# Workspace FFN: reload of x behind its residual sum, loads signalled in halves, output summed in a ring of four first rows

## The reference

```python
for _ in range(2):
    logits = rms(x, norm_pre_w) @ compete_w.T + compete_b
    vals, idx = top_k(swap(logits), 4)
    written = softmax(vals) @ gather(x @ write_w.T + write_b, idx)
    ws = rms(ws + written, norm_post_w)            # 16 slots a batch
    q = x @ wq.T + bq; kk = ws @ wk.T + bk; vv = ws @ wv.T + bv
    x = rms(x + attention(q, kk, vv) @ out_w.T + out_b, norm_post_w)
```

## Time and profile before

| | before |
|---|---|
| median of three runs | 4041.53 us |
| the profiled execution's own time | 4037.83 us |
| its span | 4036.0 us |
| mean granted TensorE clock | 0.972 of full speed |
| PE busy | 3624.9 us (90%) |
| DVE busy | 2861.6 us (71%) |
| ACT busy | 2582.2 us (64%) |
| POOL busy | 1597.4 us (40%) |
| last stage | from about 3024 us to the end |

### The profile page before, as it was taken

How to read it: one execution, slowest core, us unless ns; L and a number is a source line. 1 busy time by engine, 2 the same in 40 slices (tenths; PEclk the granted TensorE clock), 3 DMA queues, 4 the chain that set the end, 5 groups by cost and what they waited for, 6 DMA issues and landing times. The chain is left out here.

```text
span 4036.0 us, 86194 instructions
## 1 busy us (share of the span) xinstructions
PE 3624.9 (90%) x24451; PEld 1808.3 (45%) x24451; DVE 2861.6 (71%) x4477; ACT 2582.2 (64%) x6419; POOL 1597.4 (40%) x2090
## 2 busy tenths in 40 slices
PE   5999999999999996699999799999976988889896
PEld 1222222222222221577778544444444654655563
DVE  5888888888888885577777577777764455444545
ACT  2777777777777775577777577777762534445353
POOL 6444444444444440666666122222221242332323
PEclk9999999999999998799999999999998999999998
DMA  7777777777777762333333133333323030120202
GB/s 113 125 120 125 120 125 120 125 120 124 120 125 121 123 107 72 103 113 113 112 113 115 58 93 93 93 94 94 94 74 110 1 126 2 64 65 33 95 1 79
DMA packets 342550, 385.82 MB, mean 96 GB/s; under 512 B 58432, under 2 KB 223040, under 8 KB 342336
## 3 DMA queue, kind: packets, MB, share of 16 engines
q1 hardware_dynamic: 315712, 348.69, 40.2%
q10 hardware_dynamic: 26624, 34.63, 3.3%
HBM read 196.52 MB, written 84.93 MB: 70 GB/s over the span
## 5 line engine op out<-in xcount | busy, mean ns | idle before, releaser
L302 DVE TENSOR_REDUCE a_neg_max<-a_max_ps 128x2 f32<-128x1024 f32 x1024 | 1201.3, 1219 | 195.3 <-PE a_max_ps L354 171.2
L380 ACT ACTIVATE a_P<-a_ring_ps 128x512 f32<-128x512 f32 x2048 | 1084.3, 602 | 382.4 <-PE a_ring_ps L336 379.4
L354 PE MATMUL a_max_ps<-a_K,a_Q 96*128 96x512 bf16 x2048 | 621.2, 385 | 44.0 <-DMA a_K<-a_k_split 39.8
L336 PE MATMUL a_ring_ps<-a_Q,a_K 98*128 98x512 bf16 x2048 | 617.6, 382 | 6.3 <-DMA a_Q<-a_max_rows 4.1
L365 PE MATMUL a_pv_ps<-a_P,a_V 128*32 128x512 f32 x4096 | 544.9, 604 | 1.8 <-ACT a_out_sb L385 1.8
L336 PEld LDWEIGHTS a_ring_ps<-a_Q,a_K 98*128 98x128 bf16 x2048 | 159.1, 96 | 660.2 <-ACT a_P L380 585.3
L1163 ACT ACTIVATE c_P<-c_s_ps,c_bias 128x128 f32<-128x128 f32 x1024 | 362.2, 368 | 137.8 <-DVE c_bias L1035 128.6
L1092 PE MATMUL c_s_ps<-c_KD,c_qT 128*128 128x512 f32 x512 | 276.0, 621 | 33.4 <-ACT c_qT L1154 28.9
L1031 DVE TENSOR_REDUCE c_neg_max<-c_s_ps 128x4 f32<-128x512 f32 x256 | 175.5, 686 | 162.2 <-PE c_s_ps L1093 162.2
L354 PEld LDWEIGHTS a_max_ps<-a_K,a_Q 96*128 96x128 bf16 x2048 | 183.1, 98 | 220.7 <-issue 42.5
L256 POOL TENSOR_SCALAR a_var_eps<-a_mean_var 128x1 f32<-128x1 f32 x64 | 12.2, 191 | 648.4 <-DVE a_mean_var L318 648.1
(11 more groups left out here) (250 smaller groups left out, 7245.3 us busy)
## 6 DMA issues: line engine op xcount, KB each, us to landing
a_Q<-a_q_split SPq DMA_DIRECT2D x384, 128.0 KB
a_K<-a_k_split SPq DMA_DIRECT2D x384, 128.0 KB
heads_out<-a_out_sb ACTq DMA_DIRECT2D x128, 256.0 KB, 2.3
a_x_in<-in_x_dram SPq DMA_DIRECT2D x64, 256.0 KB, 3.6
a_c_in<-in_ctx_dram SPq DMA_DIRECT2D x64, 256.0 KB
a_cT_in<-in_ctxT_dram SPq DMA_DIRECT2D x64, 256.0 KB
b_x_in<-in_x_dram SPq DMA_DIRECT2D x64, 256.0 KB, 2.8
b_o_in<-heads_out SPq DMA_DIRECT2D x64, 256.0 KB
```

Source lines behind the costliest of these rows:

```text
L302: dve.tensor_reduce(neg_max[:, p, 2 * u:2 * u + 2], max_ps[u % 2][:, :, :], AX.X, ALU.max, negate=True).then_inc(max_taken, 1)
L336: pe.matmul(ring(s, use_of(k))[:, :], K[i][:, h, n:n + 128], Q[i][:, h, :], start=True, stop=True).then_inc(scores_filled, 1)
L354: last = pe.matmul(max_ps[u % 2][:, j, :], Q[i][0:KROW, h, m:m + 128], K[i][0:KROW, h, :], start=True, stop=True)
L380: act.activation(P[p][k // NT][:, k % NT, :], ring(s, use_of(k))[:, :], ACT.Exp, scale=SCALE).then_inc(exp_done, 1)
```

## The change

Three things change in the last stage, and nothing in the order in which an engine does its arithmetic but one placement.

First, `x_first` becomes a ring of four rows. POOL's sum is written into the ring and the store reads it there; `out_sb` stays a pair. `final(b)` of a second pass waits for POOL's sum of batch b-2 (`out_ready`, which starts at 2) in place of a store. `out_b_row` and `out_b_part` become names for parts of `y` and `junk2`.

Second, SP issues the reload of `X[i][:, b, :]` once `y_done` counts the residual sum of b, in front of the store of b-1. The ring's loads wait for the store four batches back.

Third, each buffer has two load semaphores, one for batches 0 to 3 and one for 4 to 7. `moments_of` takes a half; the first half is taken behind `final(7)` and ahead of `vd`, the second at the end of the step.

```diff
@@ -1282,7 +1281,8 @@
         attT = [sb(f"attT{i}", [128, NB // 2, 128]) for i in range(2)]
         VO = [sb(f"VO{i}", [128, C]) for i in range(2)]
         y, y_sq, y_ms, y_r = sb("y", [128, 2, C]), sb("y_sq", [128, 2]), sb("y_ms", [128, 1]), sb("y_r", [128, 2])
-        x_first, out_sb = sb("x_first", [128, 2, C]), sb("out_sb", [128, 2, C])
+        x_first, out_sb = sb("x_first", [128, 4, C]), sb("out_sb", [128, 2, C])
+        out_b_row, out_b_part = y[:, 0, :], junk2[0:96, :]
 
         F = [ps(f"F{i}", [128, 512]) for i in range(3)]
         SC = [ps(f"SC{i}", [128, 512]) for i in range(2)]
...
@@ -1290,9 +1290,9 @@
         xb_ps = [ps(f"xb_ps{i}", [128, 512]) for i in range(2)]
 
         small_in, big_in, const_ready, preset = sem("small_in"), sem("big_in"), sem("const_ready"), sem("preset")
-        x_loaded = [sem(f"x_loaded{i}") for i in range(2)]
-        out_stored = [sem(f"out_stored{i}") for i in range(2)]
-        x_first_loaded = [sem(f"x_first_loaded{i}") for i in range(2)]
+        x_loaded = [[sem(f"x_loaded{i}_{h}") for h in range(2)] for i in range(2)]
+        out_stored = [sem(f"out_stored{i}") for i in range(4)]
+        x_first_loaded = [sem(f"x_first_loaded{i}") for i in range(4)]
         out_ready = sem("out_ready")
         (xT_filled, xT_done, x_sq_done, x_ms_done, x_r_done, lt_filled, lt_done, l_filled, lr_done, lg_filled, lg_done) = map(
             sem, ("xT_filled", "xT_done", "x_sq_done", "x_ms_done", "x_r_done", "lt_filled", "lt_done", "l_filled", "lr_done",
...
@@ -1343,16 +1343,17 @@
                 sp.dma_start(cb_col[i * S:(i + 1) * S, :], compete_b.rearrange("(s o) -> s o", o=1)).then_inc(small_in, 16)
                 sp.dma_start(ws_in[i * S:(i + 1) * S, :], workspace).then_inc(small_in, 16)
             for dst, src in ((write_b_row, write_b), (out_b_row, out_b), (post_row, norm_post)):
-                sp.dma_start(dst[:, :], src.rearrange("(o n) -> o n", o=1).to_broadcast([128, C])).then_inc(small_in, 16)
+                sp.dma_start(dst if dst is out_b_row else dst[:, :], src.rearrange("(o n) -> o n", o=1).to_broadcast([128, C])).then_inc(small_in, 16)
             for i in range(2):
                 for b in range(NB):
-                    sp.dma_start(X[i][:, b, :], x[i * NB + b]).then_inc(x_loaded[i], 16)
+                    sp.dma_start(X[i][:, b, :], x[i * NB + b]).then_inc(x_loaded[i][b // 4], 16)
             for dst, src in ((write_sb, write_wT), (wk_sb, wkT), (wv_sb, wvT), (wq_sb, wq), (wo_sb, out_wT)):
                 sp.dma_start(dst[:, :, :], src.rearrange("(c p) n -> p c n", p=128)).then_inc(big_in, 16)
             held = Held(sp, sp_passed)
-            for i in range(2):
+            for i in range(4):
 
                 sp.sem_inc(out_stored[i], 16)
+            sp.sem_inc(out_ready, 2)
 
             def step(f, u, after):
                 if u.exists() and u.second():
@@ -1360,20 +1361,28 @@
 
                     def load_first(b):
 
-                        sp.dma_start(x_first[:, b % 2, :], x[u.eight() * NB + b]).then_inc(x_first_loaded[b % 2], 16)
-                    load_first(0)
-                    load_first(1)
+                        held.wait_ge(out_stored[b % 4], u.eight() * 32 + (b // 4 * 16 + 16))
+                        sp.dma_start(x_first[:, b % 4, :], x[u.eight() * NB + b]).then_inc(x_first_loaded[b % 4], 16)
+
+                    def store(b):
+
+                        held.wait_ge(out_ready, u.eight() * NB + (b + 3))
+                        sp.dma_start(x_out[u.eight() * NB + b], x_first[:, b % 4, :]).then_inc(out_stored[b % 4], 16)
+                    for b in range(4):
+                        load_first(b)
                     for b in range(NB):
-
-                        held.wait_ge(out_ready, u.eight() * NB + (b + 1))
-                        sp.dma_start(x_out[u.eight() * NB + b], out_sb[:, b % 2, :]).then_inc(out_stored[b % 2], 16)
-                        if b + 2 < NB:
-                            load_first(b + 2)
                         if not isinstance(u.q, int):
-                            sp.dma_start(X[i][:, b, :], x[(u.eight() + 2) * NB + b]).then_inc(x_loaded[i], 16)
+
+                            held.wait_ge(y_done, u.n() * NB + (b + 1))
+                            sp.dma_start(X[i][:, b, :], x[(u.eight() + 2) * NB + b]).then_inc(x_loaded[i][b // 4], 16)
+                        if b >= 1:
+                            store(b - 1)
+                        if 3 <= b < NB - 1:
+                            load_first(b + 1)
+                    store(NB - 1)
             units(sp, step)
-            for i in range(2):
-                sp.wait_ge(out_stored[i], 16 + 16 * B // 2)
+            for i in range(4):
+                sp.wait_ge(out_stored[i], 16 + 16 * B // 4)
 
         @block.gpsimd
         def _(pool):
@@ -1449,9 +1458,9 @@
 
                 m = u.eight() * NB + b
                 held.wait_ge(final_done, u.n() * NB + (b + 1))
-                held.wait_ge(x_first_loaded[b % 2], (u.eight() * (NB // 2) + (b // 2 + 1)) * 16)
-                pool.tensor_tensor(out_sb[:, b % 2, :], out_sb[:, b % 2, :], x_first[:, b % 2, :], ALU.add).then_inc(out_ready, 1)
-                held.wait_ge(out_ready, m + 1)
+                held.wait_ge(x_first_loaded[b % 4], (u.eight() * 2 + (b // 4 + 1)) * 16)
+                pool.tensor_tensor(x_first[:, b % 4, :], out_sb[:, b % 2, :], x_first[:, b % 4, :], ALU.add).then_inc(out_ready, 1)
+                held.wait_ge(out_ready, m + 3)
 
             def finish(u, b):
                 m = u.n() * NB + b
...
             held = Held(dve, dve_passed)
             LINKS = 6
 
-            def moments_of(f):
+            def moments_of(f, half):
 
                 e = f.eight()
-                dve.wait_ge(x_loaded[f.pair()], f.turn() * 128 + 128)
-                at_least(dve, z_done, e * NB)
-                at_least(dve, x_ms_done, f.n())
-                for b in range(NB):
+                dve.wait_ge(x_loaded[f.pair()][half], f.turn() * 64 + 64)
+                if half == 0:
+                    at_least(dve, z_done, e * NB)
+                    at_least(dve, x_ms_done, f.n())
+                for b in range(half * 4, half * 4 + 4):
                     dve.bn_stats(stats[:, b, :], X[f.pair()][:, b, :]).then_inc(stats_done, 1)
-                for b in range(NB):
+                for b in range(half * 4, half * 4 + 4):
                     held.wait_ge(stats_done, e * NB + (b + 1))
                     dve.bn_aggr(moments[:, b, :], stats[:, b, :]).then_inc(moments_done, 1)
-            moments_of(Unit(0, 0, 0))
+            moments_of(Unit(0, 0, 0), 0)
+            moments_of(Unit(0, 0, 0), 1)
@@ -1537,15 +1549,11 @@
                     m = u.n() * NB + b
                     dve.wait_ge(y_r_done, m + 1)
                     if u.second():
-                        at_least(dve, out_stored[b % 2], u_stores(u) * 64 + (b // 2 * 16 + 16))
+                        dve.wait_ge(out_ready, u.eight() * NB + (b + 1))
                         dst = out_sb[:, b % 2, :]
                     else:
                         dst = X[u.pair()][:, b, :]
                     dve.scalar_tensor_tensor(dst, y[:, b % 2, :], y_r[:, b % 2:b % 2 + 1], post_row[:, :], ALU.mult, ALU.mult).then_inc(final_done, 1)
-
-                def u_stores(u):
-
-                    return u.turn() * 2 + u.pair()
 
                 def normalise(batches):
 
@@ -1647,6 +1655,8 @@
                                       bias_cols[:, 1].unsqueeze(2).unsqueeze(3).to_broadcast([128, CK, NB, S]), ALU.add).then_inc(kd_done, 1)
                 if u.exists():
                     final(7)
+                if after.exists() and not after.second():
+                    moments_of(after, 0)
                 if f.exists():
                     dve.wait_ge(kv_filled, n * 2 + 2)
                     at_least(dve, vo_filled, (n - 1) * NB)
@@ -1655,7 +1665,7 @@
                         dve.tensor_tensor(vd[f.pair()][r, :, :, h, :], F[U_V % 3][r, :].rearrange("p (c b s) -> p c b s", c=CK, s=S),
                                           bias_cols[r, 2].unsqueeze(2).unsqueeze(3).to_broadcast([D, CK, NB, S]), ALU.add).then_inc(vd_done, 1)
                 if after.exists() and not after.second():
-                    moments_of(after)
+                    moments_of(after, 1)
             units(dve, step)
 
         @block.tensor
```

12 lines of the change are left out of this document (6 added, 6 removed).

## The result

The changed kernel takes 3989.5 us, the median of four runs (3987.1 to 3993.4), against 4040.7 before (four runs too); the ratio is 0.9873, interval 0.9856 to 0.989. The forecast was 3992 us in a range of 3982 to 4011. The profiled execution took 3987.12 us, its span 3985.3.

What follows compares the result with a forecast made beforehand. PE, which the other engines join on, was taken as the bound. A's 62.75 - 1.4 - 3.64 - 2.67 + 1.5 gave 56.5 us, B 56.7; three laps save 49.5 us, so 4041.5 becomes 3992, range 3982 to 4011.

Steps and rivals of the forecast that it cites:

- The waits that go: PE's idle for gT, before x's transposes and in the section behind them: -1.4, -3.64 and -2.67 us in A.
- the six steps: A and B over three laps of the last stage's loop: forecast 339.7 us in sum against 389.2.
- The fourth term, the halves: First four statistics ahead of vd delay PE's last group of L1817: +1.5 us a step, on the path.
- A: Even-pair step, second pass behind and new first pass ahead, between PE's L1752 marks: forecast 56.5 us from 62.75.
- my time for normalising: DVE's start of normalising x in A, behind the second four statistics and POOL's part: about 3264.8.
- The last section: PE from x's transposes (L1712) to the next L1752: 18.57 us down to 15.9, with x normalised before PE arrives.
- the reload: x reloaded once the residual sum has read it: PE's stall before the transposes goes, 10.89 to 7.25, -3.64 us.
- B: Odd-pair step of the same kind as A: forecast 56.7 us, 0.2 more than A, from 66.45.
- 1: Rival: finals lose the start to POOL's addition, 2.9 us in each of six steps, 17 us lost, 4010; chance 0.12.
- 2: Rival: first four statistics blocked by POOL's additions, vd up to 2.65 us later, 16 us, 4008; chance 0.07.
- 3: Rival: last loads of x land so late that the second four statistics wait; slower, 4054; chance 0.03.
- 4: Rival: the reload was hidden anyway, only the finals' wait and vd count, -1.4 + 1.5, no change; chance 0.02.

Runs made afterwards that it cites:

- experiment 1: All eight statistics put back behind the addition that makes vd, on the changed kernel: 3991.8 us, ratio 0.9877.
- Experiment 6: Kernel before, with 24 idle TensorE products between the scores and the transposes of x, where a new first pass follows: 4038.3 us, ratio 1.000.
- 5b: Changed kernel with POOL's three semaphore steps ahead of its addition taken out in the loop, so the addition starts sooner: 4022.8 us, ratio 0.9945.
- experiment 3: Kernel before with the early reload of x alone, no ring and no halves: 4013.3 us, ratio 0.9927.
- experiment 4: Changed kernel with POOL's two operations for ws moved ahead of its addition of batch 3: 3999.9 us, ratio 0.9894.
- 4b: Changed kernel with POOL's two ws operations ahead of its addition of batch 3 and all eight statistics behind vd: 3995.6 us, ratio 0.9881.

## Why the prediction was right

*The waits that go.* The finals' wait for stores and the statistics' wait for x are gone, and the six steps come to 339.45 us for 339.7 forecast. By PE's landmarks: mark to L1791 (was L1781) 8.99 us for 10.22, -1.23 (forecast -1.4: PE's idle there is 1.67 us, not 1.49); L1710 to L1722 7.25, -3.64 (as forecast); L1722 to the mark 15.96, -2.61 (forecast -2.67).

*The fourth term, the halves, is mis-sized, and it isn't on the path.* From L1791 to L1710 it was 23.07 us and is 24.21, 1.14 more where I had 1.5. `vd` is 0.90 of it. The rest is `ws`: L1791 to L1802 takes 8.95 us for 8.61, since POOL's two small operations for it stand behind an addition that now takes 1.64 us beside the final (it ends just ahead of 3242.64) and took 1.27 before; I had no term for that. But experiment 1 shows that the 0.90 costs nothing: without it the scores end sooner and TensorE waits for `att` instead. I had added landmarks of PE as if PE set each of them.

*The working that would have been right was in my rows.* From the first normalising to the next mark it was 3288.74 - 3269.57 = 19.17 us already, and this is what stays. With my time for normalising, 3264.8 or 38.8 us behind the mark (my own terms, 3262.1 + 2.4, make it 3264.5), that gives 58.0 us for A, 1.5 over what I forecast, and some 4001 us for the kernel, the edge of my own range. What came is 37.25 + 19.16. I had left POOL's `y_r` of batch 7 at its old place, 28.4 us behind the mark; without the finals' waits ahead of it it came at 27.1 (3253.13 + 0.55 against 3226.55), and the statistics with it. So the forecast of 56.5 was met by a sum whose parts on PE are right in size, while what sets them came 1.6 us sooner than the text had it. That the waits go and what this is worth on PE was foreseen; that it comes out within 0.1 us a step is in part luck, for the sum of PE's parts and my own time of normalising didn't agree.

*The last section.* I took 15.9 us for it, because x would be normalised before PE arrives, and not because of the clock. Experiment 6 supports that reading for before: 18.57 us at either clock.

*The parts overlap.* My terms gave 3.64 us a step to the reload; alone it gives 29.2 / 6 = 4.9, the ring alone 5.1, both 8.3. The sum was made for both together, and only for both does it hold. B's 3.7 us over A went, as I had assumed; before, its products behind the wait for `gT` took 5.37 us at the low clock where A's took 3.67, so part of this was the clock.

*The rivals.* 1 didn't come: every final of the second passes in the loop takes 0.75 us, VectorE starting 0.25 us ahead of POOL (3240.46 and 3240.71). Its mechanism is real (5b) and its price was too low, 33 us in place of 17. 2 didn't come: four statistics take 2.46 us beside POOL's addition at 3254.05, 0.61 each, as the eight before did (4.85). That agrees with the rule of the Trainium skill, SBUF — State Buffer, section Who interferes with whom, that a VectorE instruction with one SBUF input, outside the 2-port modes, does not contend with GpSimd. 3 didn't come: the second four statistics start without a wait. 4 falls with experiment 3, where the reload by itself is worth 28 us.

*Elsewhere.* The last two units kept their 1.86 us finals, as said. The plain step of the first lap took 56.84 us for 58.38; its granted clock is 1.00 throughout, where 0.83 had been granted over ten microseconds of it (3385 to 3395); those 1.5 us are more than the 0.9 that the six steps don't explain, and nothing that I forecast.

## What to carry to other kernels

When two engines meet at the end of a step, don't add up landmarks of the busier one: split the step at the event that both need (here the first normalised rows) and look which half changes; a half that stays at 19.17 us in nine of twelve kernels, whatever was changed ahead of it, says that the gain lies in the other. How near the second engine is shows only when it is made late: 1.8 us on TensorE lengthened that half by 1.15 (experiment 4). A wait removed there is worth its length only until the next engine is late, and two edits on one chain overlap, so size them together or measure each alone. On an in-order engine that makes small values for another (POOL's `y_r`), look for large operations that stand ahead of them and could stand behind: one such move gave 1.26 us a step, and three semaphore steps that let the other engine start first gave 8.7 us at the end.

## What the runs showed of the hardware

A final with two SBUF inputs (`y` and `post_row`) and POOL's addition get in each other's way by who starts first: with the final 0.24 us or more ahead, it takes 0.75 us and the addition 1.55 to 1.64; within 0.05 us of each other, 1.77 to 1.86 and 1.26. The Trainium skill, SBUF — State Buffer, section Who interferes with whom, says that issue order decides who blocks. From 0.24 us of lead the traces agree; at the end of the changed kernel VectorE's start is recorded 0.05 us ahead (3974.13 and 3974.18) and it is the final that is long, so a lead that small doesn't tell who goes first. What I hadn't expected is that three semaphore steps on POOL (0.08 to 0.37 us from the end of `y_r`) are enough to turn it.

TensorE's granted clock fell behind a wait of 1.81 us in experiment 4 (64 products in 8.67 us for 7.41), and not behind the 0.90 us of the changed kernel; it is 1.2 GHz in part of such a stretch. In 4b it fell in the first lap and not in the second behind the same waits, and in experiment 3 in the second lap and not in the third, behind the same wait of 2.91 us. Behind the late x the lower clock cost nothing (experiment 6); behind `gT` 1.4 to 2.0 us a step, and behind `vd` in experiment 4 most of 1.4.
